# The row of attention scores, moved from in front of the second product to behind it in TensorE's queue

## The chip, the cores and the metric

The kernel runs on one core of one Trainium2 chip. The metric is the device time of one execution in microseconds (us), as the median of several runs. The engines are named as the profile names them: PE is TensorE (its weight loads are listed apart, as PEld), DVE is VectorE, ACT is ScalarE, POOL is GpSimd and SP is SyncE, which issues transfers here.

## What is computed

Four layers stand one behind the other, each with a residual, on an input of 4 batches x 512 rows x 256 columns. The third takes nearly all the arithmetic, the fourth holds the step that is moved.

```python
x = x + L0(x, itok_8)     # adapter 256 -> 64 -> 256, layer norm
x = x + L1(x, itok_7)     # one 256 x 256 product
x = x + L2(x, itok_2)     # five two-layer nets 256 -> 1024 -> 256, gated
x = x + L3(x, itok_2)     # attention pooling

# L2: two chosen experts, mixed with two weights, and three shared nets
dense(x, wi, wo) = relu(x @ wi) @ wo

# L3
attn_in = tanh(hidden @ W1 + b1)          # 512 x 64
scores  = attn_in @ v                     # 512
masked  = where(mask, scores[None, :], -1e30)   # prefix, suffix or all but itself
p       = softmax(masked)
out     = (p @ hidden) / count(mask)
```

## The kernel before

**Precision.** Each factor of a product is split in a high and a low part (names ending in `_hi` and `_lo`), and a product is the sum of three matmuls: high by low, high by high, low by high. So a product over 256 rows of contraction, with 512 columns, is six matmuls.

**Slots.** A batch is worked off in 40 slots (`SLOTS`), one for each 128 hidden units of the five nets. In slot q PE computes the first product of chunk q (`first_product`, six matmuls into `ps_hid`, lines 801, 802, 806), then whatever small steps of other layers belong to the slot, and then the second product of chunk q-2 (`second_product`, six matmuls into `ps_net`, lines 858, 859, 863). ACT turns the first product into `hid_hi` (line 1068) and DVE into `hid_lo` (line 1705). There are three banks for the hidden chunks, so the first product of chunk q waits for `hid_lo` of chunk q-3.

**The small steps.** While batch b goes through its slots, the layers 0 and 1 of batch b+1 (`stage_a`) and the attention of batch b-1 (`stage_c`) are threaded in. The table `C_SLOT` says in which slot each step of the attention stands: the hidden layer of the attention in slot 10, its split in slot 11 (DVE lines 1386 and 1388, which write `att_split`), the row of scores in slot 12, and then on DVE a copy of the scores in column form (lines 1393 and 1396), a running maximum from either side in slots 13 and 14, and so on. The products that need the exponents stand in slots 19, 21 and 22. The attention of the last batch, and the last steps of the one before it, have code of their own behind the loop (`last_rows`).

**The row of scores.** These are two matmuls of 512 columns into `ps_side`, lines 689 and 690. The first contracts over 64 partitions (`att_split[0:A]` with A = 64, against the low part of v), the second over 128 (all of `att_split`, against the high part of v). In front of them stands a wait on DVE for `att_lo`, the end of line 1388. DVE's line 1393 waits for the second. The step is run three times: during the batches 1, 2 and 3, for the batches 0, 1 and 2.

**What sets the order.** Nothing is scheduled. Each engine works its own queue in the order in which the code is written out, and waits on semaphores that count finished steps of other engines. A wait holds everything behind it on its engine. Before the change PE's order in slot 12 is first product of chunk 12, row of scores, second product of chunk 10.

Of the kernel before, what the change touches and what calls it, by code (L numbers as in the profile page):

```python
# [31 lines left out]
def cond_resid_program(  # L32
# [56 lines left out]
    with ExitStack() as ctx:  # L89
# [196 lines left out]
        def score_banks(final):  # L286

            rows = (ps_net[:, 0, 0:HS], ps_hid[:, 0, 0:HS]) if final else (ps_side[:, 1],)
            return rows, ps_hid[:, 2]
# [31 lines left out]
        def ring(b, q):  # L321
            return (b * SLOTS + q) % HB
# [145 lines left out]
        def _(pe):  # L468
# [212 lines left out]
                    product_both(ps_side[:, 0], att_w_st, (c_dve.sem, c_dve.at(i, "x3lo1"))).then_inc(c_pe.sem, 1)  # L681
                attention(slot, i, False)

            def attention(slot, i, final):

                if slot == C_SLOT["scores"]:
                    row = score_banks(False)[0][0]
                    pe.wait_ge(c_dve.sem, c_dve.at(i, "att_lo"))
                    mm(row, att_v_lo[:], att_split[0:A], start=True, stop=False)
                    mm(row, att_v_hi[:], att_split[:], start=False, stop=True).then_inc(c_pe.sem, 1)  # L690
                if slot == (LATE_TSUM if i == LATE else C_SLOT["tsum"]):
                    tile_sums(i, False)
                if 0 <= slot - C_SLOT["out"] < 2 and i != LATE:
                    t = 2 * (slot - C_SLOT["out"])
                    pooled((t, t + 1), i, "loop")
# [7 lines left out]
            def tile_sums(i, final):  # L703


                pe_s, _, dve_s, n = c_steps(i, final)
                _, vh, vl = c_buffers(final)
                pe.wait_ge(dve_s.sem, dve_s.at(n, "edge_lo"))
                if final:
                    pe.wait_ge(e_pool.sem, e_pool.at(0, "val_lo1"))  # L710
                for t in range(R):
                    st = edge_st[:, t * P:(t + 1) * P]
                    mm(tsum_bank(final), st, vh[:, t], start=(t == 0), stop=False)
                    last = mm(tsum_bank(final), st, vl[:, t], start=False, stop=(t == R - 1))
                last.then_inc(pe_s.sem, 1)

            def pooled(tiles, i, mode):


                final = mode == "final"  # L720
                f, half = int(final), tiles[0] // 2
                pe_s, _, dve_s, n = c_steps(i, final)
                _, vh, vl = c_buffers(final)
                part = str(half) if final else ""
                pe.wait_ge(dve_s.sem, dve_s.at(n, "phi" + part if final else "tsum_lo"))
                for t in tiles:
                    if tiles[0] == 2 and mode == "loop":
                        pe.wait_ge(dve_s.sem, dve_s.at(n, f"out{t - 2}"))
                    mm(out_bank(t, mode), prob_hi[:, f, tile_cols(t)], vh[:, t], start=True, stop=False)
                    mm(out_bank(t, mode), prob_hi[:, f, tile_cols(t)], vl[:, t], start=False, stop=False)  # L730
                if final:
                    pe.wait_ge(e_dve.sem, e_dve.at(0, f"plo{half}"))
                for t in tiles:
                    mm(out_bank(t, mode), prob_lo[:, f, tile_cols(t)], vh[:, t], start=False, stop=False)
                if final:
                    pe.wait_ge(e_dve.sem, e_dve.at(0, "tsum_lo"))
                    pe.wait_ge(e_pool.sem, e_pool.at(0, f"wgt_lo{half}"))
                else:
                    pe.wait_ge(c_dve.sem, c_dve.at(n, "wgt_lo"))
                for t in tiles:  # L740
                    mm(out_bank(t, mode), wgt_st[:, f, tile_cols(t)], tsum[:, f], start=False, stop=True).then_inc(pe_s.sem, 1)

            def last_gates(slot):

                if slot == END_GATE:
                    pe.wait_ge(gate_in, 32)
                    pe.wait_ge(gate_sum.sem, gate_sum.at(B - 1, "g2k1"))
                    pe.wait_ge(c_dve.sem, c_dve.at(LATE, "tsum_lo"))
                    pe.wait_ge(e_act.sem, e_act.at(0, "last0"))
                    gate_columns(True).then_inc(e_pe.sem, 1)  # L750
                if slot == END_GATE + 1:
                    pe.wait_ge(e_act.sem, e_act.at(0, "gate_h"))
                    gate_logits().then_inc(e_pe.sem, 1)
# [55 lines left out]
            def bank_free(b, net, k):  # L809


                if k == 1 and (net > 0 or b > 0):
                    by, i, name = evac_act, (b if net > 0 else b - 1), f"g{(net - 1) % NG}"
                elif k == 0 and (net >= 2 or b > 0):
                    by, i, name = evac_dve, (b if net >= 2 else b - 1), f"g{(net - 2) % NG}"
                else:
                    return
                pe.wait_ge(by.sem, by.at(i, name))

            def second_product_halved(b, q):  # L820

                net, tiles, c = NG - 1, chunks(q, True), q % (CH // 2)
                w, half = tiles[0][0] % RING, int(q > HALF0_END)
                if c == 0:
                    bank_free(b, net, half)

                def term(wo, hid, n, k, start=False, stop=False):
                    return mm(ps_net[:, GROUP_BANKS[net][half], k * HS:(k + 1) * HS], wo[:, w, n, k * P:(k + 1) * P], hid[:, ring(b, q), tiles[n][3]],  # L830
                              start=start, stop=stop, skip_group_check=True)

                pe.wait_ge(hid_hi_ready, b * SLOTS + q + 1)
                if split_by_vector(b, tiles[0][0]):
                    pe.wait_ge(end_wo_lo_ready, tiles[0][0] - PAIRS + 3)
                for n in range(2):
                    for k in range(KD):
                        term(wo_hi, hid_hi, n, k, start=(c == 0 and n == 0 and k == 0))
                        term(wo_lo, hid_hi, n, k)
                pe.wait_ge(hid_lo_ready, b * SLOTS + q + 1)  # L840
                for n in range(2):
                    for k in range(KD):
                        last = term(wo_hi, hid_lo, n, k, stop=(c == CH // 2 - 1 and n == 1))
                last.then_inc(net_chunk_done, 1)

            def second_product(b, q, first, halved):

                if halved and q >= SLOTS - CH:
                    return second_product_halved(b, q)
                net, slot = GROUP_AT[q // CH], ring(b, q)  # L850
                opens, closes = q == GROUP_FIRST[net], q == GROUP_END[net] - 1
                pe.wait_ge(hid_hi_ready, b * SLOTS + q + 1)
                w = (q // 2) % RING
                for k in range(KD):
                    if opens:
                        bank_free(b, net, k)
                    cols, dst = slice(k * P, (k + 1) * P), ps_net[:, GROUP_BANKS[net][k]]
                    mm(dst, wo_hi[:, w, q % 2, cols], hid_hi[:, slot], start=opens, stop=False)  # L858
                    mm(dst, wo_lo[:, w, q % 2, cols], hid_hi[:, slot], start=False, stop=False)  # L859
                pe.wait_ge(hid_lo_ready, b * SLOTS + q + 1)  # L860
                for k in range(KD):
                    cols, dst = slice(k * P, (k + 1) * P), ps_net[:, GROUP_BANKS[net][k]]
                    last = mm(dst, wo_hi[:, w, q % 2, cols], hid_lo[:, slot], start=False, stop=closes)  # L863
                last.then_inc(net_chunk_done, 1)

            def batch(b, first, last):
                for q in range(SLOTS):
                    first_product(b, q, first, last)
                    if not first and (not last or q < C_SLOT["out"] or q == LATE_TSUM):
                        stage_c(q, b - 1)  # L870
                    if not last:
                        stage_a(q, b + 1, not first)
                    if last and q == END_GATE:
                        last_gates(q)
                    for s in second_slots(q, last):
                        second_product(b, s, first, last)
                    if last and q == END_GATE:
                        last_gates(q + 1)
                if last:
                    second_product(b, SLOTS - 1, first, last)  # L880
# [1008 lines left out]
```

## Time and profile before

| | |
|---|---|
| median of 3 runs | 525.22 us |
| lowest and highest of them | 524.85, 525.82 us |
| the profiled execution's own time | 524.68 us |
| its span, first to last instruction | 522.9 us |
| mean granted clock of PE | 0.993 |
| PE busy | 509.9 us, 98% of the span |
| PE weight loads | 422.9 us, 81% |
| DVE, ACT, POOL busy | 63%, 51%, 46% |

The profiled execution took 524.68 us, of which 1.8 us lie outside its span. It is 0.54 us below the median. A busy time of PE is not a measure of its useful work here, since the records of neighbouring matmuls overlap. What tells whether PE moved on is the distance from the start of one matmul to the start of the next, and rows of a timeline are read that way below.

### The profile page before, as it was taken

To read this page: it belongs to the slowest core of one execution; us is meant where nothing else is said; L and a number is where in the kernel's file an instruction comes from. 1 tells how busy PE (TensorE), PEld (TensorE's weight loads), DVE (VectorE), ACT (ScalarE), POOL (GpSimd) and SP (SyncE) were. 2 spreads that over 40 slices of the span, in tenths; PEclk is the share of its full clock that TensorE was granted. 3 is DMA by queue.
4 is the path that set the end of the run, shared out by engine and by line. 5 is a ranking of instruction groups with operands and counts; after the bars stand their busy time and mean duration, and the time that the engine had idled before them with its cause. 6 is when DMAs were issued, how large, how long until landed. Compare 5 with 4: busy or idle time off the path is not lost.

```text
span 522.9 us, 7047 instructions
## 1 busy us (share of the span) xinstructions
PE 509.9 (98%) x2463; PEld 422.9 (81%) x2465; DVE 329.5 (63%) x606; ACT 266.1 (51%) x508; POOL 238.5 (46%) x205
## 2 busy tenths in 40 slices
PE   8899999999999999999999999999999999999986
PEld 5688888888888788888888788888888878888974
DVE  7688224884676674786467675687367676435386
ACT  4565554443557563545266564445355647444253
POOL 2655455445344443443535433434544434734034
PEclk9999999999999999999999999999999999999997
DMA  5624442222224323323143422322222223420002
GB/s 172 202 107 132 104 137 102 81 81 81 81 81 131 102 80 88 132 66 113 52 137 97 145 89 81 121 81 80 81 81 81 80 81 104 139 81 1 1 0 81
DMA packets 44539, 49.31 MB, mean 94 GB/s; under 512 B 7380, under 2 KB 34264, under 8 KB 44504
## 3 DMA queue, kind: packets, MB, share of 16 engines
q1 hardware_dynamic: 42888, 47.03, 28.0%
q10 hardware_dynamic: 1616, 1.84, 1.0%
q8 instruction: 20, 0.33, 0.3%
q14 instruction: 15, 0.12, 0.1%
HBM read 46.76 MB, written 2.10 MB: 93 GB/s over the span
## 4 chain that ended last, share of the span: by engine, by line
PE 91%; DVE 5%; ACT 2%; ACTq 1%; POOL 1%; issue 1%; DVEq 0%
PE ps_hid L801 14%; PE ps_hid L806 13%; PE ps_hid L802 13%; PE ps_net L858 13%; PE ps_net L859 13%; PE ps_net L863 13%; PE ps_net L830 2%; PE ps_side L554 1%; PE ps_side L662 1%; PE ps_side L478 1%; PE ps_side L482 1%; PE ps_side L477 1%; DVE att_split L1386 1%; PE ps_side L488 1%; PE ps_side L491 1%; PE ps_side L530 1%
## 5 line engine op out<-in xcount | busy, mean ns | idle before, releaser
L1705 DVE SCALAR_TENSOR_TENSOR hid_lo<-ps_hid,hid_hi 128x512 fp32r<-128x512 f32 x160 | 110.4, 690 | 165.8 <-ACT hid_hi L1068 164.8
L1801 POOL TENSOR_TENSOR wi_lo<-raw_wi,wi_hi 128x512 fp32r<-128x512 f32 x78 | 104.1, 1334 | 225.3 <-ACT wo_hi L1049 121.2
L1068 ACT ACTIVATE hid_hi<-ps_hid 128x512 fp32r<-128x512 f32 x160 | 95.4, 597 | 208.9 <-PE ps_hid L806 208.2
L801 PE MATMUL ps_hid<-x2T_hi,wi_lo 128*128 128x512 f32 (+1 forms) x332 | 125.9, 381 | 0.3 <-POOL wi_lo L1799 0.3
L802 PE MATMUL ps_hid<-x2T_hi,wi_hi 128*128 128x512 f32 (+1 forms) x332 | 125.3, 380 | 0.0
L858 PE MATMUL ps_net<-hid_hi,wo_hi 128*128 128x512 f32 x304 | 120.8, 397 | 0.0
L859 PE MATMUL ps_net<-hid_hi,wo_lo 128*128 128x512 f32 x304 | 118.8, 391 | 0.0
L1802 POOL TENSOR_TENSOR wo_lo<-raw_wo,wo_hi 128x512 fp32r<-128x512 f32 x78 | 101.5, 1301 | 0.0
L806 PE MATMUL ps_hid<-x2T_lo,wi_hi 128*128 128x512 f32 (+1 forms) x332 | 99.1, 380 | 0.0
L863 PE MATMUL ps_net<-hid_lo,wo_hi 128*128 128x512 f32 x304 | 93.9, 390 | 0.0
L801 PEld LDWEIGHTS ps_hid<-x2T_hi,wi_lo 128*128 128x128 f32 x332 | 62.4, 188 | 12.4 <-POOL wi_lo L1799 0.5
L802 PEld LDWEIGHTS ps_hid<-x2T_hi,wi_hi 128*128 128x128 f32 x332 | 62.5, 188 | 11.7
L806 PEld LDWEIGHTS ps_hid<-x2T_lo,wi_hi 128*128 128x128 f32 x332 | 61.3, 188 | 11.8
L863 PEld LDWEIGHTS ps_net<-hid_lo,wo_hi 128*128 128x128 f32 x304 | 57.1, 188 | 12.2
L859 PEld LDWEIGHTS ps_net<-hid_hi,wo_lo 128*128 128x128 f32 x304 | 57.2, 188 | 10.7
L858 PEld LDWEIGHTS ps_net<-hid_hi,wo_hi 128*128 128x128 f32 x304 | 57.2, 188 | 10.7
L1042 ACT ACTIVATE wi_hi<-raw_wi 128x512 fp32r<-128x512 f32 x79 | 49.3, 624 | 0.8 <-PE ps_net L863 0.8
L1049 ACT ACTIVATE wo_hi<-raw_wo 128x512 fp32r<-128x512 f32 x47 | 29.2, 622 | 0.0
L1046 ACT ACTIVATE wo_hi<-raw_wo,par 128x512 fp32r<-128x512 f32 x32 | 22.9, 715 | 1.1 <-DVE mix_done L1539 1.1
L1047 ACT ACTIVATE raw_wo<-raw_wo,par 128x512 f32<-128x512 f32 x32 | 22.8, 712 | 0.0
L1303 DVE SCALAR_TENSOR_TENSOR x3T<-netT,gates,x3T 128x512 f32<-128x512 f32 x24 | 19.6, 855 | 0.1
L1693 DVE SCALAR_TENSOR_TENSOR gate_acc<-gate_w,netT,gate_acc 128x256 f32<-128x256 f32 x26 | 17.5, 672 | 2.1 <-DVE gate_acc L1690 0.5
(324 smaller groups left out, 532.2 us busy)
## 6 DMA issues: line engine op xcount, KB each, us to landing
raw_wi<-in_L_cond_share_wi_dram SPq DMA_DIRECT2D x23, 512.0 KB, 3.7
raw_wo<-in_L_cond_share_wo_dram SPq DMA_DIRECT2D x23, 512.0 KB, 4.8
raw_wi<-in_L_cond_expert_wi_dram SPq DMA_DIRECT2D x16, 512.0 KB, 3.7
raw_wo<-in_L_cond_expert_wo_dram SPq DMA_DIRECT2D x16, 512.0 KB, 4.7
x_rows<-in_x_dram SPq DMA_DIRECT2D x3, 512.0 KB, 5.9
out_dram<-out_rows SPq DMA_DIRECT2D x6, 256.0 KB, 5.1
gate_w<-in_L_cond_gate_w_dram SPq DMA_DIRECT2D x1, 1024.0 KB, 5.5
subj_w<-in_L_cond_weight_dram SPq DMA_DIRECT2D x3, 256.0 KB, 2.7
```

The lines of the kernel that those rows point to most:

```text
L801: mm(dst, wi_lo[:, w, k, c], x2T_hi[:, k, rows], start=(k == 0), stop=False)
L802: mm(dst, wi_hi[:, w, k, c], x2T_hi[:, k, rows], start=False, stop=False)
L806: last = mm(dst, wi_hi[:, w, k, c], x2T_lo[:, k, rows], start=False, stop=(k == KD - 1))
L858: mm(dst, wo_hi[:, w, q % 2, cols], hid_hi[:, slot], start=opens, stop=False)
L859: mm(dst, wo_lo[:, w, q % 2, cols], hid_hi[:, slot], start=False, stop=False)
L863: last = mm(dst, wo_hi[:, w, q % 2, cols], hid_lo[:, slot], start=False, stop=closes)
L1042: fn(wi_hi[:, w], raw_wi[:, half % 2, :, c], ACT.Copy)
L1049: fn(wo_hi[:, w], raw, ACT.Copy).then_inc(w_hi_ready, 1)
L1068: fn(hid_hi[:, ring(b, q)], ps_hid[:, ring(b, q)], ACT.Relu).then_inc(hid_hi_ready, 1)
L1705: v.scalar_tensor_tensor(out=hid_lo[:, ring(b, q)], in0=ps_hid[:, ring(b, q)], scalar=0.0, in1=f32(hid_hi[:, ring(b, q)]), op0=ALU.max, op ...
L1801: g.tensor_tensor(wi_lo[:, w], raw_wi[:, half % 2, :, c], f32(wi_hi[:, w]), ALU.subtract)
L1802: g.tensor_tensor(wo_lo[:, w], raw_wo[:, half % 2, t], f32(wo_hi[:, w]), ALU.subtract).then_inc(w_lo_ready, 1)
```

## The change

The two matmuls and their wait are taken out of `attention` and put into a function of their own. `attention` was called from `stage_c`, ahead of the second product of the slot. The new function is called behind it. The condition `if not first` runs it for the batches 1, 2 and 3, as before. No instruction is added or removed, and no other engine's code is touched.

```diff
-            def attention(slot, i, final):
-
+            def score_row(slot, i):
                 if slot == C_SLOT["scores"]:
                     row = score_banks(False)[0][0]
                     pe.wait_ge(c_dve.sem, c_dve.at(i, "att_lo"))
                     mm(row, att_v_lo[:], att_split[0:A], start=True, stop=False)
                     mm(row, att_v_hi[:], att_split[:], start=False, stop=True).then_inc(c_pe.sem, 1)
+
+            def attention(slot, i, final):
+
...
                     for s in second_slots(q, last):
                         second_product(b, s, first, last)
+                    if not first:
+                        score_row(q, b - 1)
                     if last and q == END_GATE:
                         last_gates(q + 1)
```

PE's queue in slot 12 of batch 1, before the change. In brackets stand the semaphores that an instruction waits for: `c_dve` counts DVE's steps of the attention, `hid_hi_ready` and `hid_lo_ready` the halves of the hidden chunks.

```order
L806 MATMUL ps_hid<-x2T_lo,wi_hi 128x512 x2
L689 MATMUL ps_side<-att_split,att_v_lo 128x512 [waits c_dve]
L690 MATMUL ps_side<-att_split,att_v_hi 128x512
L858 MATMUL ps_net<-hid_hi,wo_hi 128x512 [waits hid_hi_ready]
L859 MATMUL ps_net<-hid_hi,wo_lo 128x512
L858 MATMUL ps_net<-hid_hi,wo_hi 128x512
L859 MATMUL ps_net<-hid_hi,wo_lo 128x512
L863 MATMUL ps_net<-hid_lo,wo_hi 128x512 [waits hid_lo_ready]
L863 MATMUL ps_net<-hid_lo,wo_hi 128x512
L801 MATMUL ps_hid<-x2T_hi,wi_lo 128x512 [waits hid_lo_ready]
```

The same place after the change, where the line numbers are those of the new file (806 has become 808, 689 has become 688, 858 has become 860, 801 has become 803).

```order
L808 MATMUL ps_hid<-x2T_lo,wi_hi 128x512 x2
L860 MATMUL ps_net<-hid_hi,wo_hi 128x512 [waits hid_hi_ready]
L861 MATMUL ps_net<-hid_hi,wo_lo 128x512
L860 MATMUL ps_net<-hid_hi,wo_hi 128x512
L861 MATMUL ps_net<-hid_hi,wo_lo 128x512
L865 MATMUL ps_net<-hid_lo,wo_hi 128x512 [waits hid_lo_ready]
L865 MATMUL ps_net<-hid_lo,wo_hi 128x512
L688 MATMUL ps_side<-att_split,att_v_lo 128x512 [waits c_dve]
L689 MATMUL ps_side<-att_split,att_v_hi 128x512
L803 MATMUL ps_hid<-x2T_hi,wi_lo 128x512 [waits hid_lo_ready]
```

The two matmuls of the row have gone past six matmuls of the second product. They now stand between the second product of chunk 10 and the first product of chunk 13.

DVE's queue at the end of slot 11, in slot 12 and at the start of slot 13, which is the same before and after the change but for line numbers (these are of before).

```order
L1386 CAST att_split<-attT 64x512 [waits c_act]
L1388 TENSOR_TENSOR att_split<-attT,att_split 64x512 [waits c_dve]
L1705 SCALAR_TENSOR_TENSOR hid_lo<-ps_hid,hid_hi 128x512 [waits hid_hi_ready]
L1393 TENSOR_TENSOR prob<-ps_side,ident 128x512 [waits c_pe]
L1396 TENSOR_REDUCE score_col<-prob 128x4 [waits c_dve]
L1705 SCALAR_TENSOR_TENSOR hid_lo<-ps_hid,hid_hi 128x512 [waits hid_hi_ready]
```

Nothing moved there. Line 1393 waits for the row of scores, and behind it in the queue stands `hid_lo` of chunk 13.

## Rows read from the trace of the kernel before

**Rows 1.** The page, part 1: busy us of each engine, share of span, instructions.
```profile
PE 509.9 (98%) x2463; PEld 422.9 (81%) x2465; DVE 329.5 (63%) x606; ACT 266.1 (51%) x508; POOL 238.5 (46%) x205
```
**Rows 2.** What PE waited for, 60 to 480 us: total us, times, longest.
```profile
PE ps_side L689 <- DVE att_split L1388: 1.2, 3, 0.4
```
**Rows 3.** Timeline, PE, slot 12 of batches 1 and 3: start us, duration us, line.
```profile
171.76 0.61 PE L806 MATMUL ps_hid<-x2T_lo,wi_hi 128*128 128x512 f32 x2
172.76 0.50 PE L689 MATMUL ps_side<-att_split,att_v_lo 64*128 64x512 f32 x1 [0.39 <-DVE att_split L1388]
173.19 0.50 PE L690 MATMUL ps_side<-att_split,att_v_hi 128*128 128x512 f32 x1
173.53 0.39 PE L858 MATMUL ps_net<-hid_hi,wo_hi 128*128 128x512 f32 x1
...
418.43 0.62 PE L806 MATMUL ps_hid<-x2T_lo,wi_hi 128*128 128x512 f32 x2
...
420.19 0.39 PE L858 MATMUL ps_net<-hid_hi,wo_hi 128*128 128x512 f32 x1
```
**Rows 4.** Timeline, weight loads, slot 12 of batch 1.
```profile
172.76 0.18 PEld L689 LDWEIGHTS ps_side<-att_split,att_v_lo 64*128 64x128 f32 x1 [0.81 <-DVE att_split L1388]
173.19 0.19 PEld L690 LDWEIGHTS ps_side<-att_split,att_v_hi 128*128 128x128 f32 x1 [0.25 <-issue]
173.30 0.19 PEld L858 LDWEIGHTS ps_net<-hid_hi,wo_hi 128*128 128x128 f32 x1
```
**Rows 5.** Timeline, DVE, slots 11 to 13 of batch 1.
```profile
172.02 0.69 DVE L1388 TENSOR_TENSOR att_split<-attT,att_split 64x512 fp32r<-64x512 f32 x1
...
173.73 0.69 DVE L1393 TENSOR_TENSOR prob<-ps_side,ident 128x512 f32<-128x512 f32 x1
174.45 0.69 DVE L1396 TENSOR_REDUCE score_col<-prob 128x4 f32<-128x512 f32 x1
177.16 0.69 DVE L1705 SCALAR_TENSOR_TENSOR hid_lo<-ps_hid,hid_hi 128x512 fp32r<-128x512 f32 x1 [2.02 <-ACT hid_hi L1068]
```
**Rows 6.** Timeline, PE, the second product of chunk 13 (slot 15).
```profile
181.71 0.39 PE L858 MATMUL ps_net<-hid_hi,wo_hi 128*128 128x512 f32 x1
...
182.62 0.62 PE L863 MATMUL ps_net<-hid_lo,wo_hi 128*128 128x512 f32 x2
```
**Rows 7.** Timeline, PE, a restart after a wait between matmuls of equal partitions.
```profile
483.20 0.39 PE L801 MATMUL ps_hid<-x2T_hi,wi_lo 128*128 128x256 f32 x1 [0.30 <-POOL wi_lo L1799]
483.42 0.28 PE L802 MATMUL ps_hid<-x2T_hi,wi_hi 128*128 128x256 f32 x1
483.54 0.28 PE L801 MATMUL ps_hid<-x2T_hi,wi_lo 128*128 128x256 f32 x1
```
**Rows 8.** Timeline of the last stage, PE and weight loads: four transposes in two surroundings.
```profile
502.35 0.60 PE L662 MATMUL ps_side<-ident,x3T 128*128 128x128 f32 x4
502.70 0.37 PE L729 MATMUL ps_net<-val_hi,prob_hi 128*128 128x258 f32 x1
...
506.76 0.66 PE L662 MATMUL ps_side<-ident,x3T 128*128 128x128 f32 x4
507.35 1.05 PE L700 MATMUL ps_hid<-att_v,attT 64*128 64x1 f32 x8
...
506.76 0.42 PEld L662 LDWEIGHTS ps_side<-ident,x3T 128*128 128x128 f32 x4 [0.33 <-issue]
507.35 0.96 PEld L700 LDWEIGHTS ps_hid<-att_v,attT 64*128 64x128 f32 x8 [0.17 <-issue]
```
**Rows 9.** Stretches: busy PE, PEld, DVE, ACT, POOL; granted clock, DMA. Then PE's timeline.
```profile
508.00:509.00 1.00, 0.40 (x4) 0.31 (x3) 0.96 (x3) 0.62 (x3) 0.54 (x1) 0.89 0.00 0
515.00:516.00 1.00, 1.00 (x6) 0.40 (x4) 0.90 (x4) 1.00 (x4) 0.86 (x2) 0.70 0.00 0
...
510.29 0.42 PE L730 MATMUL ps_net<-val_lo,prob_hi 128*128 128x258 f32 x1
510.50 0.42 PE L729 MATMUL ps_net<-val_hi,prob_hi 128*128 128x258 f32 x1
```

## The prediction, made before the changed kernel was run

> **What bounds the kernel now.** I read the shares of busy time first. PE is busy for 509.9 of 522.9 us, and no other engine passes 63% [rows 1]. So PE's queue sets the time of the loop, and only what makes that queue longer or shorter counts there. The next view is the list of what PE waited for. Between 60 and 480 us, which is nearly the whole of the four batches, it holds one entry: line 689, the first matmul of the row of scores, waits for DVE's line 1388, three times, 1.2 us in all [rows 2]. The reader should see two things. Every other transfer and every other engine is early enough throughout the loop, so there is no second wait standing close behind this one in the list. And what can be won by curing this wait is small.
>
> The list understates the loss, because it counts only the gap between the modelled end of one matmul and the start of the next. The timeline gives the true loss by starts. A matmul of 512 columns in the steady stream starts 0.2275 us after the one before: from the first matmul of line 858 at 181.71 to line 863 at 182.62 are four steps [rows 6]. In slot 12 the first of the two matmuls of line 806 starts at 171.76, and line 858 starts at 173.53 [rows 3]. Between them lie four steps, two of line 806 and two of the row, which at the steady pace would be 0.91 us. They took 1.77 us, 0.86 us too long. The third occurrence reads 418.43 to 420.19, which is 1.76 us, 0.85 too long [rows 3], and the second lies between. So slot 12 loses 0.86 us in each of three batches, 2.6 us in all.
>
> **Where the 0.86 us go.** They fall into parts, and the change touches them differently.
>
> The first part is the wait. Line 689 should start two steps after 171.76, at 172.22, and starts at 172.76 [rows 3], 0.54 us late. DVE's line 1388 ends at 172.02 + 0.69 = 172.71 [rows 5], and the matmul starts 0.05 us after. This is a genuine wait on DVE.
>
> The second part lies behind the wait. Line 690 starts 0.43 us after line 689, and line 858 starts 0.34 us after line 690 [rows 3], in place of 0.23 each: 0.20 and 0.11 us too much, 0.31 together. Some of that belongs to any restart. Where PE restarts after a wait between two matmuls of 128 partitions, the next one comes 0.22 us after it and the following one 0.12 us later [rows 7], so a restart costs 0.10 us, the time in which the weight load lies bare. The remaining 0.21 us are not explained by the restart. They belong to the step from 64 partitions to 128. The weight load of line 690 is not issued while line 689 runs: it stands 0.25 us idle for want of issue, and starts at 173.19 together with its matmul [rows 4], where in the steady stream a load runs one step ahead, as that of line 858 does, at 173.30 for a matmul at 173.53. I read it as 0.10 us of standing still before the load and 0.11 us of bare load.
>
> **The change, part by part.**
>
> *The wait.* In the new place the row comes six matmuls later. The second product of chunk 10 starts at 172.22, since its inputs are two chunks old, and takes 6 x 0.2275 = 1.37 us, so the row is due at 173.58. DVE's line 1388 ends at 172.71, because nothing ahead of it moves. The cover is 173.58 - 172.71 = 0.87 us, and even a weight load issued one step early, at 173.35, finds its data. The wait of 0.54 us goes, three times: -1.62 us. If the cover were gone, the wait would return at its own length, at most the 0.54 us that it has now.
>
> *The restart.* With no wait, the bare load that follows a wait would go too, 0.10 us a time. But it goes only if the load of line 689 may be issued early, and that is the open question, because line 689 uses 64 partitions and stands behind matmuls of 128.
>
> *Going from 128 partitions to 64.* Before the change this price could not be seen, since it lay under the wait. It is now on PE's path. The nearest rows are in the last stage. Four transposes between matmuls of 128 partitions take 0.35 us from their first start to the next matmul (502.35 to 502.70), and the same four between matmuls of 64 partitions take 0.59 us (506.76 to 507.35) [rows 8]. The load behind them stands idle 0.17 us for want of issue, with no wait in the code there. Of the 0.24 us, 0.10 are the bare first load, and 0.14 are lost in going over to 64 partitions. The way back in slot 12 lost 0.10 before its load [rows 4]. So the price is 0.10 to 0.14 us. Its bounds are zero below, if the load is issued early, and 0.33 us above, the idle time of the load at 506.76 [rows 8], which stands behind a slower kind of matmul. I take 0.10 us, the value of this very pair of matmuls. The bare load behind it is then the 0.10 us that the restart costs today, so that term stays.
>
> *Going back from 64 to 128.* Behind line 690 now stands line 801 where line 858 stood. Both are matmuls of 128 partitions with their data ready. The 0.21 us stay as they are: 0.
>
> The Trainium skill has a rule on this. "TensorEngine Tiling (Array Packing)", section Key Properties, says that a change of the tiling mode, and not merely of the tile, drains TensorE. By that rule the row pays at both ends wherever it stands and the forecast below holds; without it the sum would be 0.1 us or more a batch better. The idle loads on both sides of the 64-partition matmuls agree with it.
>
> *DVE.* The row now ends later. In slot 12 it started at 172.76 and starts at 173.58 + 0.10 = 173.68, which is 0.92 us later, and DVE's lines 1393 and 1396 follow it: they end at 174.45 + 0.69 + 0.92 = 176.06. Behind them stands `hid_lo` of chunk 13, which before the change started at 177.16 after 2.02 us of idle time [rows 5], and which now can start 0.44 us earlier, at 176.72. So DVE keeps 0.66 us of idle time there and passes nothing on. All later steps of the attention stand behind a `hid_lo` in DVE's queue and keep their distance to PE.
>
> *The rest.* ACT, POOL, SP and all transfers are paced by PE's finished chunks, and none was late before. They move forward together with PE. The stall of 0.30 us at 483.20 [rows 7] waits for a split on POOL whose own start hangs on a finished chunk, and so keeps its length.
>
> **The sum.** For each batch -0.54 (wait) + 0.10 (over to 64 partitions) = -0.44 us; three batches -1.3 us. The slot lies in the loop, on PE, and PE leads to the last stage, so all of it should reach the end. The profiled execution would go from 524.68 to 523.4 us, its span from 522.9 to 521.6. Taken from the median of the runs, 525.22, the forecast is 523.9 us, 0.25% less.
>
> **The rivals.**
>
> *A. No price for 64 partitions.* All that is lost in slot 12 is a consequence of the wait. Then 0.86 us a batch are won, 2.6 us in all: 522.6 us. With only the entry free, the gain is 0.64 a batch: 523.3 us. For it speaks that the 0.31 us have never been seen apart from a wait. Against it speaks the 0.59 against 0.35 us of the transposes [rows 8]. Chance 0.12.
>
> *B. A higher price.* At the upper bound of 0.33 us a batch, 3 x 0.21 = 0.6 us are left: 524.6 us. The row that gives this bound stands behind matmuls of another kind. Chance 0.12.
>
> *C. The last stage gives it back.* Near the end PE's granted clock falls to half, to 1.2 GHz, when PE idles: it is 0.89 in the stretch of 508 to 509 us, in which PE is busy for 0.40 us, and back on its way up at 0.70 in that of 515 to 516 [rows 9]. In between a matmul of 258 columns starts 0.21 us after the last [rows 9] instead of 0.12 us. Were the return to full clock bound to elapsed time and not to the work, the work would come 1.3 us earlier against it, and some or all of the last 16 matmuls, two pairs of tiles with 8 each, would run at half clock: 8 to 16 x 0.09 = 0.7 to 1.4 us back, to 524.6 to 525.3, say 524.9 us. The spread of the runs, 524.85 to 525.82 us, may already contain it, in which case it changes no median. Chance 0.12.
>
> *D. The change does not do what it says.* The wait would have to last on in the new place, or PE to find another of the same length behind it. The queues show the row behind the second product, the cover is 0.87 us, and no other wait is in the list [rows 2]. It would give 525.2 us. Chance 0.05.
>
> *E. Slower.* DVE now waits longer for the row, with `hid_lo` of chunk 13 behind that wait. If this made `hid_lo` late, PE's second product of chunk 13 would stand. Before, `hid_lo` ended at 177.85 and was needed at 182.62 [rows 5, 6], 4.8 us later, and 2.0 us of idle time lie before it. It decides from a delay of some 6 us, against 0.9 us that I find. Were the delay one slot more than that, 2.7 us in each batch, the time would be 525.2 + 8.2 - 1.6 = 531.8 us. Chance 0.04.
>
> **How the numbers follow.** The forecast has 0.55, A 0.12, B 0.12, C 0.12, D 0.05, E 0.04. The range leaves out the far half of A, and D and E but for their edge: 523.1 to 525.0 us. A measurement of this kernel can tell about 0.2% from no change, which is 1.05 us, so faster means below 524.17. The forecast is 0.27 us beyond that line; I give 0.50 of its 0.55 to faster, add A, and have 0.62. Same gets the other 0.05, B, C and D: 0.34. Slower gets E: 0.04.
>
> **What would show it.** In the list of what PE waited for, the row's entry is gone and nothing new of this size has come. In PE's timeline the second product starts 0.23 us after the last matmul of the first, and the row's first matmul 0.33 us after the last of the second product (0.23 would be A, 0.56 would be B), its second 0.43 us after that, and line 801 of the next chunk 0.34 us later (both 0.23 in A). The load of the row's first matmul shows idle time for want of issue. DVE's line 1393 waits for the row and 1396 ends about 0.7 us before the next `hid_lo`. The stretches of half clock near the end have the same place relative to the work; if they do not, C is at work. The prediction is wrong if the row's surroundings lose more than 0.5 us a batch, or if the loop ends 1.3 us earlier and the kernel does not.

## The result, and the profile after

| | before | after |
|---|---|---|
| median | 525.34 us (6 runs) | 523.63 us (6 runs) |
| lowest and highest | 524.85, 525.82 us | 523.46, 524.20 us |
| span of the profiled execution | 522.9 us | 521.4 us |
| mean granted clock | 0.993 | 0.993 |

The ratio of the times is 0.9968 with a 95% interval from 0.9957 to 0.9980. The change makes the kernel faster by 1.7 us, or 0.32%, and the interval of 1.1 to 2.3 us holds the 1.3 us of the forecast. The median of 523.63 us lies 0.3 us below the 523.9 us of the forecast, inside its range of 523.1 to 525.0 us.

In the changed file the row of scores has the lines 688 and 689, the first product 803, 804 and 808, the second 860, 861 and 865. PE's timeline in slot 12 of batch 1, which answers to [rows 3], reads as follows (start us, duration us, line):

```profile
173.00 0.61 PE L865 MATMUL ps_net<-hid_lo,wo_hi 128*128 128x512 f32 x2
173.55 0.49 PE L688 MATMUL ps_side<-att_split,att_v_lo 64*128 64x512 f32 x1
173.97 0.50 PE L689 MATMUL ps_side<-att_split,att_v_hi 128*128 128x512 f32 x1
174.31 0.39 PE L803 MATMUL ps_hid<-x2T_hi,wi_lo 128*128 128x512 f32 x1
```

From the first matmul of line 865 to line 803 are four steps, which at the steady pace of 0.2275 us take 0.91 us. They took 1.31 us, 0.40 too long. Before, the four steps around the row were 0.86 us too long. The row's first matmul should start at 173.455 and starts 0.10 us late. The next steps are 0.42 and 0.34 us; before they were 0.43 and 0.34.

The list of what PE and its weight loads waited for, 60 to 480 us, shows no entry of PE any more in place of [rows 2]. It has three entries of the weight loads (total us, times, longest), of which the last two are the row's:

```profile
PEld ps_side L554 <- DVE norm L1217: 1.3, 3, 0.4
PEld ps_side L688 <- issue: 1.1, 3, 0.4
PEld ps_side L689 <- issue: 0.7, 3, 0.2
```

"Issue" means that no semaphore explains the idle time: the data of line 688 were ready, and its load was still not sent ahead. On DVE, against [rows 5], the row is now waited for, and the idle time ahead of `hid_lo` of chunk 13 has shrunk from 2.02 to 0.67 us without being used up:

```profile
171.91 0.69 DVE L1392 TENSOR_TENSOR att_split<-attT,att_split 64x512 fp32r<-64x512 f32 x1
...
174.51 0.69 DVE L1397 TENSOR_TENSOR prob<-ps_side,ident 128x512 f32<-128x512 f32 x1 [0.83 <-PE ps_side L689]
175.24 0.69 DVE L1400 TENSOR_REDUCE score_col<-prob 128x4 f32<-128x512 f32 x1
176.59 0.69 DVE L1709 SCALAR_TENSOR_TENSOR hid_lo<-ps_hid,hid_hi 128x512 fp32r<-128x512 f32 x1 [0.67 <-ACT hid_hi L1072]
```

Where the 1.5 us between the two spans come from can be read from the start of the same matmul in both traces. Line 806 of slot 12 in batch 1 starts at 171.76 in [rows 3] and its counterpart at 171.65: 0.11 us arise in the part ahead of any changed instruction. That is chance: over all profiles of this document, in which PE's work up to there is the same, the start lies between 171.62 and 171.92 us. The first transposes of the last stage start at 502.35 in [rows 8] and now here:

```profile
500.86 0.60 PE L662 MATMUL ps_side<-ident,x3T 128*128 128x128 f32 x4
```

That is 1.49 us earlier. Less the 0.11 us, three slots gave 1.38 us, 0.46 each, which is 0.86 - 0.40. From there on both take 20.5 us to the end of the span.

### The profile page after: what moved, and what is told of

It reads as the page before. It is cut to its first block, busy times and chain, and to the rows that moved or that the text cites. A ratio compares the mean times of both kernels' runs of the same rounds, so it can differ in the third digit from the quotient of the medians.

```text
span 521.4 us, 7049 instructions
## 1 busy us (share of the span) xinstructions
PE 509.6 (98%) x2465; PEld 422.3 (81%) x2465; DVE 329.8 (63%) x606; ACT 266.1 (51%) x508; POOL 238.5 (46%) x205
## 4 chain that ended last, share of the span: by engine, by line
PE 93%; DVE 3%; ACT 1%; ACTq 1%; POOL 1%; issue 0%; DVEq 0%
PE ps_hid L803 14%; PE ps_hid L808 14%; PE ps_hid L804 14%; PE ps_net L860 13%; PE ps_net L861 13%; PE ps_net L865 13%; PE ps_net L832 2%; PE ps_side L554 1%; PE ps_side L662 1%; PE ps_side L478 1%; PE ps_side L482 1%; PE ps_side L477 1%; PE ps_side L488 1%; PE ps_side L491 1%; PE ps_side L530 1%
```

## The experiments

The theory after the result: the wait of 0.54 us is gone, and what is left of the row's loss, 0.40 us a batch, is the price of going from matmuls over 128 partitions to one over 64 and back. Rivals are that the place itself matters, that the loss has another cause, and that DVE's lateness has a price.

The ratios below are against runs of the kernel before that were made beside each experiment. Their medians are 525.34 us for the first four experiments, 524.99 us for those with five pairs or ten grouped matmuls, and 525.15 us for the last, with matmuls on zeros.

**The row's first matmul over 128 partitions.** The low part of v gets zeros in its upper 64 partitions, and the matmul reads all of `att_split`. The sums stay the same.

```diff
-        att_v_lo = sb("att_v_lo", [A, P], F32R)
+        att_v_lo = sb("att_v_lo", [P, P], F32R)
...
-                    mm(row, att_v_lo[:], att_split[0:A], start=True, stop=False)
+                    mm(row, att_v_lo[:], att_split[:], start=True, stop=False)
...
+            v.memset(f32(att_v_lo[A:P]), 0.0)
```

> The changed kernel, with the row's first matmul over 128 partitions instead of 64: the low part of v is padded with zeros in the upper 64, so the count of matmuls and the sums stay as they are. Theory (in the changed kernel 0.40 us a batch are lost because the array goes from 128 partitions to 64 and back): both idle loads vanish, the row's matmuls start 0.23 us apart like all others, and 3 x 0.40 = 1.2 us are won over the changed kernel: 522.4 us, ratio to the kernel before 0.9944. Rival (the loss comes from something else about the row, its place, its bank or its operands): 523.6 us, ratio 0.9968, and the 0.10, 0.20 and 0.11 us stay.

Measured: 522.73 us (6 runs), ratio 0.9948, interval 0.9936 to 0.9961. In slot 12 nothing is lost any more:

```profile
173.09 0.61 PE L865 MATMUL ps_net<-hid_lo,wo_hi 128*128 128x512 f32 x2
173.54 0.39 PE L688 MATMUL ps_side<-att_split,att_v_lo 128*128 128x512 f32 x1
173.78 0.39 PE L689 MATMUL ps_side<-att_split,att_v_hi 128*128 128x512 f32 x1
174.01 0.39 PE L803 MATMUL ps_hid<-x2T_hi,wi_lo 128*128 128x512 f32 x1
```

The four steps take 0.92 us, and the loads' two entries for the row are gone from the list. The last stage begins at 499.64 us, 1.22 us earlier than in the changed kernel, as the theory has it. The rival is out. The time fell by only 0.9 us and the span by 0.5; the last part of this section comes back to that.

**The same padding with the row in its old place**, in front of the second product.

> The kernel before, with the row in its old place but with 128 partitions in both of its matmuls (low part of v padded with zeros). It separates the wait from the change of partitions. Theory: the wait of 0.54 us and the bare load of the restart, 0.10 us, stay, the 0.21 us behind them go: 3 x 0.21 = 0.65 us less than before, 524.7 us, ratio 0.9988. Rival A (all that is lost in slot 12 follows from the wait): as before, 525.3 us, with 0.43 and 0.34 us between the starts. Rival (padding does not help): the same.

Measured: 524.92 us (11 runs), ratio 0.9993, interval 0.9984 to 1.0002. The time alone, which fits the forecast of 0.9988, doesn't tell it from no change. The trace does:

```profile
171.92 0.61 PE L806 MATMUL ps_hid<-x2T_lo,wi_hi 128*128 128x512 f32 x2
172.92 0.50 PE L689 MATMUL ps_side<-att_split,att_v_lo 128*128 128x512 f32 x1 [0.39 <-DVE att_split L1388]
173.26 0.39 PE L690 MATMUL ps_side<-att_split,att_v_hi 128*128 128x512 f32 x1
173.49 0.40 PE L858 MATMUL ps_net<-hid_hi,wo_hi 128*128 128x512 f32 x1
```

The wait is the old one: line 689 starts 0.54 us behind its time. The step after it is 0.34 us, 0.11 more than the pace, and the next one 0.23. So a restart costs 0.11 us, and the 0.21 us of before that are missing here belong to the partitions. From line 806 of slot 12 in batch 1 to the last stage this kernel takes 330.03 us (171.92 to 501.95), the kernel before 330.59 us (171.76 to 502.35), so 0.56 us went where 0.65 were expected. Rival A of the prediction, in which everything followed from the wait, is out.

**The row one slot later, in its old position between the two products.**

```diff
-                if slot == C_SLOT["scores"]:
+                if slot == C_SLOT["scores"] + 1:
```

> The kernel before, with the row in its old position between first and second product, but one slot later, 13 instead of 12, so that DVE has long finished its part. It takes the wait away without going behind the second product. Theory (only the wait counted, the place does not): as the changed kernel, 523.6 us, ratio 0.9968, 0.40 us lost in slot 13. DVE gets the row 1.4 us later than in the changed kernel, hid_lo of chunk 13 comes about 0.7 us late and PE does not notice, since it has 4.8 us. Rival (lateness on DVE already costs, or the place behind the second product is itself of worth): 524.5 us or more.

Measured: 523.60 us (6 runs), ratio 0.9968, interval 0.9956 to 0.9980, the same as the changed kernel. The four steps around the row, from 174.44 to 175.74, take 1.30 us. `hid_lo` of chunk 13 starts at 177.27 on DVE, 0.7 us later than in the changed kernel, with no idle time ahead of it:

```profile
177.27 0.68 DVE L1705 SCALAR_TENSOR_TENSOR hid_lo<-ps_hid,hid_hi 128x512 fp32r<-128x512 f32 x1
```

PE waits for nothing between 60 and 480 us. So the gain lies in asking for `att_lo` later, and the place behind the second product has no worth of its own.

**The row three slots later, between the two products of slot 15.** The edit is the same with `+ 3`.

> The kernel before, with the row between first and second product of slot 15, three slots late, so that hid_lo of chunk 13 is queued on DVE behind a wait for a row that stands right ahead of the matmuls which need it. It tests the slower rival of the prediction. Theory: the row ends about 7 us after its time in the changed kernel; hid_lo of chunk 13 ends 1.4 us after PE's line 863 of that chunk asks for it; with the restart 1.5 us are lost a batch, 4.4 in all, over the 523.6 us of the changed kernel: 528.0 us. Rival (DVE's lateness passes nothing to PE): 523.6 us. Rival (it also makes ACT late in slot 16 and costs a second stall): 530 us or more.

Measured: 527.97 us (2 runs), ratio 1.0045, interval 1.0028 to 1.0063. PE's waits from 60 to 490 us, the line of interest:

```profile
PE ps_net L863 <- DVE hid_lo L1705: 3.5, 3, 1.2
```

PE's timeline in slot 15 of batch 1:

```profile
180.82 0.50 PE L690 MATMUL ps_side<-att_split,att_v_hi 128*128 128x512 f32 x1
...
181.86 0.39 PE L859 MATMUL ps_net<-hid_hi,wo_lo 128*128 128x512 f32 x1
183.43 0.73 PE L863 MATMUL ps_net<-hid_lo,wo_hi 128*128 128x512 f32 x2 [1.18 <-DVE hid_lo L1705]
184.00 0.40 PE L801 MATMUL ps_hid<-x2T_hi,wi_lo 128*128 128x512 f32 x1
```

DVE's timeline there shows its wait for the row, and `hid_lo` of chunk 13 behind it, which ends at 183.37:

```profile
181.36 0.69 DVE L1393 TENSOR_TENSOR prob<-ps_side,ident 128x512 f32<-128x512 f32 x1 [7.63 <-PE ps_side L690]
...
182.69 0.68 DVE L1705 SCALAR_TENSOR_TENSOR hid_lo<-ps_hid,hid_hi 128x512 fp32r<-128x512 f32 x1
```

Line 863 starts 1.34 us behind its time (183.43 - 181.86 - 0.23) and the step after its pair is 0.11 us too long: 1.45 us a batch, 4.4 in all. The last stage begins at 505.20 against 500.86 us, 4.34 us later. So the slower rival of the prediction is a real mechanism with the size that the queue of DVE gives. It costs nothing one slot later than the original place and 1.45 us a batch three slots later; in between nothing was run. An estimate from these rows: line 690 comes 7.7 us later than in the kernel before (180.82 against 173.19, with 0.06 us for the earlier start of slot 12 here), and 1.34 us of that reach PE, so the loss would begin at a delay of about 6.3 us.

**The price of a pair by itself.** The row is computed five times in a row, with 64 and 128 partitions in turn, and the same with 128 throughout.

```diff
+                    for _ in range(4):
+                        mm(row, att_v_lo[:], att_split[0:A], start=True, stop=False)
+                        mm(row, att_v_hi[:], att_split[:], start=False, stop=True)
                     mm(row, att_v_lo[:], att_split[0:A], start=True, stop=False)
```

> The changed kernel with the row computed five times in a row, each time a matmul over 64 partitions and one over 128. It measures the price of a pair by itself. Theory (each passage between 64 and 128 partitions keeps the next weight load from running ahead): a further pair costs 0.455 us of steady pace and 0.31 us of lost time or more, up to 0.42; four further pairs in three batches 12 x 0.77 to 12 x 0.87 = 9.2 to 10.4 us: 532.8 to 534.1 us. Rival (lost time comes only once per row): 12 x 0.455 = 5.5 us, 529.1 us.

> The same with 128 partitions in every matmul (low part of v padded with zeros). Theory: the steady pace alone, 12 x 0.455 = 5.5 us over the padded kernel with one row, 522.4 + 5.5 = 527.9 us. Rival (the row's matmuls are slow for another reason): as the kernel with five unpadded pairs, 533 us.

Measured: 534.91 us (2 runs), ratio 1.0186, interval 1.0156 to 1.0215, for pairs of 64 and 128; 528.04 us (3 runs), ratio 1.0055, interval 1.0033 to 1.0078, for 128 throughout. Two steps of the first, then three of the second:

```profile
174.05 0.50 PE L690 MATMUL ps_side<-att_split,att_v_hi 128*128 128x512 f32 x1
174.48 0.49 PE L689 MATMUL ps_side<-att_split,att_v_lo 64*128 64x512 f32 x1
174.90 0.50 PE L690 MATMUL ps_side<-att_split,att_v_hi 128*128 128x512 f32 x1
```

```profile
174.03 0.39 PE L689 MATMUL ps_side<-att_split,att_v_lo 128*128 128x512 f32 x1
174.25 0.40 PE L690 MATMUL ps_side<-att_split,att_v_hi 128*128 128x512 f32 x1
174.49 0.39 PE L689 MATMUL ps_side<-att_split,att_v_lo 128*128 128x512 f32 x1
```

A matmul over 64 partitions behind one over 128 starts 0.43 us after it, and so does one over 128 behind one over 64; between equal ones it is 0.23 us. A passage costs 0.20 us, a pair 0.85 us. Twelve further pairs would be 10.2 us. The last stage begins 10.35 us later than in the changed kernel. The median lies 11.3 us above that kernel's and 0.8 us above the expected range. The profiled execution spent 21.5 us in its last stage instead of 20.5, of which more below. The kernel with 128 partitions throughout came out at 528.04 us where 527.9 was expected, and its last stage begins 5.64 us later than in the padded kernel with one row.

**Ten matmuls, two passages.** The same ten matmuls a batch as in the first of these, grouped: four over 128 partitions, five over 64, one over 128.

```diff
+                    for _ in range(4):
+                        mm(row, att_v_hi[:], att_split[:], start=True, stop=True)
+                    for _ in range(4):
+                        mm(row, att_v_lo[:], att_split[0:A], start=True, stop=True)
```

> The changed kernel with the same ten matmuls as in the five pairs, but grouped: four over 128 partitions, then five over 64, then one over 128. Theory (what costs is the passage, not a matmul over 64 partitions): only two passages a batch as in the changed kernel, so eight further matmuls at steady pace, 12 x 0.455 = 5.5 us: 529.1 us. Rival (every matmul over 64 partitions loses time): as the five pairs, 533 us.

Measured: 528.77 us (3 runs), ratio 1.0071, interval 1.0047 to 1.0096. The five matmuls over 64 partitions (line 691 four times, then 692) and their neighbours:

```profile
173.53 1.09 PE L689 MATMUL ps_side<-att_split,att_v_hi 128*128 128x512 f32 x4
174.54 1.21 PE L691 MATMUL ps_side<-att_split,att_v_lo 64*128 64x512 f32 x4
175.59 0.39 PE L692 MATMUL ps_side<-att_split,att_v_lo 64*128 64x512 f32 x1
175.92 0.50 PE L693 MATMUL ps_side<-att_split,att_v_hi 128*128 128x512 f32 x1
176.25 0.39 PE L807 MATMUL ps_hid<-x2T_hi,wi_lo 128*128 128x512 f32 x1
```

From 173.53 to 176.25 are ten steps, 2.28 us at the steady pace, in 2.72 us. The 0.44 us too much are nearly the 0.40 of a single row, though five matmuls run over 64 partitions. It is the passage that costs, and not the matmul over 64.

Not every change in the number of partitions has this price. In the kernel before, matmuls over 97 and over 128 partitions, with 256 columns, stand in turn elsewhere, and they start 0.12 us apart, as those with 256 columns over 128 partitions do in [rows 7]:

```profile
99.05 0.28 PE L516 MATMUL ps_side<-w_lo,hT_hi 97*128 97x256 f32 x1
99.17 0.29 PE L517 MATMUL ps_side<-w_hi,hT_both 128*128 128x256 f32 x1
99.30 0.28 PE L516 MATMUL ps_side<-w_lo,hT_hi 97*128 97x256 f32 x1
```

**The last stage.** In its profile the padded kernel had won 1.22 us by the start of its last stage and only 0.5 us in its span. Two kernels were profiled once more, unaltered.

> The padded kernel with the row behind the second product once more, for a second look at its last stage. In its first profile the half-clock stretch began 5.4 us after the last stage's first matmul over 64 partitions, in the kernel before and the changed one after 3.3 us, and the last stage took 21.3 us in place of 20.5. Theory (where the half-clock stretch falls is chance of the execution, not a trait of the kernel): either picture may come; if the early one comes (3.3 us, last stage 20.5 us), the span is 520.2 us. Rival (the row's earlier end always shifts the work against the clock): the late one again, span 520.9 us.

> The changed kernel, unaltered, once more, for a second look at slot 12 and at the last stage. Theory: slot 12 to the hundredth as in its first profile (0.40 us lost a batch); last stage 20.5 us with the clock falling 3.3 us after the first matmul over 64 partitions, or, by chance, 21.3 us with it falling at 5.4 us. Rival: the same picture of the clock each time.

Measured, with the start of the first transposes of the last stage, the length from there to the end of the span, and the places where PE's granted clock falls to its half, 1.2 GHz, and where it is full again:

| kernel | last stage starts | length | clock falls | full again | span | time |
|---|---|---|---|---|---|---|
| before | 502.35 | 20.5 | 508.8 | 515.6 | 522.9 | 524.68 |
| changed | 500.86 | 20.5 | 507.3 | 514.2 | 521.4 | 524.20 |
| changed, again | 500.82 | 20.8 | 508.2 | 515.0 | 521.6 | 523.49 |
| padded | 499.64 | 21.3 | 508.1 | 514.9 | 520.9 | 522.71 |
| padded, again | 499.75 | 20.8 | 506.9 | 513.8 | 520.5 | 522.30 |

The loop is the same to 0.1 us from one execution to the next: in its second profile the changed kernel again needs 1.30 us for the four steps around the row. The last stage is not the same. The next rows are PE's restart after its 1.5 us of idle time, and the stretches between 507 and 509 us, in the padded kernel. Behind the stretch stand its length, the busy times of PE, PEld, DVE, ACT and POOL with their counts, and then the granted clock. The first profile:

```profile
507.20 0.39 PE L731 MATMUL ps_net<-val_hi,prob_hi 128*128 128x258 f32 x1 [1.51 <-ACT norm L1020]
...
507.00:508.00 1.00, 0.80 (x6) 0.80 (x7) 0.93 (x4) 0.15 (x1) 0.68 (x1) 1.00 0.00 0
508.00:509.00 1.00, 0.60 (x4) 0.31 (x2) 0.90 (x6) 0.20 (x1) 0.00 (x0) 0.54 0.00 0
```

The second:

```profile
507.30 0.58 PE L731 MATMUL ps_net<-val_hi,prob_hi 128*128 128x258 f32 x1 [1.51 <-ACT norm L1020]
...
507.00:508.00 1.00, 0.70 (x3) 0.70 (x4) 0.93 (x4) 0.25 (x1) 0.78 (x1) 0.50 0.00 0
508.00:509.00 1.00, 1.00 (x7) 1.00 (x6) 0.90 (x6) 0.21 (x1) 0.00 (x0) 0.50 0.00 0
```

The work in these two is at the same place to 0.1 us, and the clock falls 1.1 us apart. The places are worked out from the mean in a stretch, with 1.00 ahead of the fall and 0.50 behind it: 0.54 granted between 508 and 509 us puts the fall at 508.1 in the first profile, and 0.97 granted between 506 and 507 us puts it at 506.9 in the second. In the two profiles of the changed kernel it falls 0.9 us apart.

The table shows two things more. Where the clock falls later it is also full again later, by the same amount to 0.1 us, though the work has not moved: 0.8 us between the profiles of the changed kernel, 1.1 us between those of the padded one. And the later in the last stage the clock is full again, the longer the stage: 13.3 us into it in the first two rows, then 14.2, 15.3 and 14.0, with lengths of 20.5, 20.5, 20.8, 21.3 and 20.8 us. So the length differs between executions of one kernel, by 0.3 and 0.5 us in these two. Over all the profiles it lies between 20.5 and 21.5 us, and the 21.3 and 21.5 of two kernels with five pairs are of this kind too, full again at 15.5 and 15.7 us. Expected was one of two pictures; the second profiles showed two others between them, so the choice of two was wrong. What sets the point of the fall was not settled.

A single profile is therefore a poor measure of the whole time. The spans of all runs, not only the profiled ones, have medians of 523.1 us before (the 17 runs beside the first experiments), 521.7 us changed and 520.6 us padded. By spans the change gives 1.4 us and the padding 1.1 us more, which fit the 1.38 and 1.22 us that the traces show in the loop. The times scatter more than the spans, since 1.8 to 2.9 us lie outside the span.

To see whether PE's idle time causes the fall, seven matmuls on zeros were put into it, on top of the padding.

```diff
                 score_columns(col, e_pe)
+                keep_warm(7, ps_hid[:, 1])
                 pe.wait_ge(e_act.sem, e_act.at(0, "late1"))
```

> The padded kernel with the row behind the second product, and seven matmuls on zeros in the last stage, ahead of the pooling of the last but one batch, where PE stands idle for 1.5 us waiting on ACT. They fill that idle time at 0.21 us each. Theory (PE's idle time there is what makes its clock fall to half): the half-clock stretch vanishes or begins later, matmuls of 258 columns behind it start 0.12 us apart instead of 0.21, and the last stage takes 20.0 to 20.5 us in every run: 521.7 to 522.3 us, with a smaller spread than 1 us. Rival (the fall has another cause, or DVE alone sets the last stage): no change against the padded kernel, 522.7 us, with the same spread.

Measured: 522.36 us (4 runs, 522.06 to 522.64), ratio 0.9947, interval 0.9930 to 0.9964. The granted clock by stretches, and PE's longest wait that is left there:

```profile
505.00:512.00 7.00, 6.00 (x38) 4.14 (x38) 6.28 (x19) 4.78 (x15) 3.60 (x5) 1.00 0.00 0
512.00:516.00 4.00, 2.81 (x17) 1.98 (x15) 3.77 (x11) 1.53 (x5) 3.19 (x4) 0.99 0.22 70
516.00:520.00 4.00, 0.00 (x0) 0.00 (x0) 1.24 (x5) 0.00 (x0) 0.00 (x0) 0.50 0.59 197
...
509.50 0.39 PE L715 MATMUL ps_net<-wi_hi,edge_st 128*128 128x258 f32 x1 [1.00 <-DVE edge_st L1373]
```

The clock stays full until PE has no work left. All four runs show it: their mean granted clock is 0.996 to 0.999, against 0.991 to 0.993 in the padded kernel's six. The matmuls of 258 columns start 0.12 us apart. So the fall hangs on that idle time of 1.5 us; the 1.0 us of idle time that is left, up to 509.50, brought none.

The time hardly shows it. The last stage took 20.6 us in the profile, for PE now waits for DVE, 1.0 us there and 0.8 us in three later waits, where the padded kernel's first profile has one such wait, of 0.8 us. Both the time and the last stage are 0.1 us above what was expected. Against the runs beside them the two kernels are not told apart, with ratios of 0.9947 and 0.9948. The spread of the times is 0.6 us in 4 runs against 2.1 us (522.02 to 524.11) in 6, but one run makes up more than half of the 2.1, and without it the spread is 0.9 us. That the spread became smaller is not shown.

## Why the prediction was right

**The wait.** The sum rested on 0.54 us of wait in each of three batches, read from starts and not from the listed idle time of 0.39. All three are gone. The cover was 0.85 us (line 1392 ends at 172.60, the row is due at 173.455), where 0.87 was worked out.

**The price that could not be seen before.** For going from 128 to 64 partitions the prediction took 0.10 us from the way back of the same pair, between bounds of 0 and 0.33. The changed kernel shows 0.10. The four extra pairs show that both directions cost the same, 0.20 us with the bare load. That agrees with what the prediction cites from the Trainium skill, "TensorEngine Tiling (Array Packing)", section Key Properties, that a change of mode drains TensorE: ten grouped matmuls with two passages lose 0.44 us, and five alternating pairs with ten passages lose 1.99 us (173.08 to 177.80, less twelve steps of 0.2275). That a drain is what holds the load back, by 0.10 us, is a reading of the page's rule; the runs show only that the load comes late.

**The term that stays.** The 0.31 us behind the wait were split into 0.10 for the restart and 0.21 for the partitions, from one restart elsewhere [rows 7]. The padded row in its old place showed just this: 0.11 for the restart, and the rest gone.

**DVE.** Lines 1397 and 1400 ended 0.67 us ahead of the next `hid_lo`; 0.66 was worked out.

**The rivals.** A, no price for 64 partitions, is refuted by the padded row in both places. B, a price of 0.33 us, is refuted by the 0.10 in the trace. C, the half clock in the last stage, has a sound core: the return to full clock moved with the fall and not with the work, and a later return went with a longer stage. What C left out is that the fall itself moves, by 0.9 and 1.1 us between executions of the same kernel. In the two profiles that were compared, fall and return came at the same work, and that both last stages took 20.5 us is luck. D is out, since PE's list of waits is empty. E is a real mechanism, with a price of 1.45 us a batch three slots late, and its threshold of some 6 us is 6.3 by the estimate above. The 531.8 us given for E take off the whole wait of 1.6 us and leave out the 0.3 us that the forecast adds for the entry; with them it is 532.1.

**The size.** Forecast was 1.3 us, measured 1.7 with an interval of 1.1 to 2.3 us. The trace gives 1.38 us in the three slots, 0.46 each instead of 0.44. The difference of 1.7 us between the medians of the times is larger than what the loop gives, and by the medians of the spans it is 1.4 us. The 0.3 us between the two would then lie outside the span, which varies between executions, and they are within the interval. The profiled execution of the changed kernel shows this scatter best: it has the shortest span of the six, 521.4 us, and the longest time, 524.20 us. That the measured 1.7 us agree with the 1.3 us as they do rests on the loop for 1.4 us and on chance for the rest.

## What to carry to other kernels

On an engine that is otherwise always busy, a wait of half a microsecond can be cured by asking later, if the work that moves ahead of it is ready and the engine that gets the result later has idle time ahead of its next urgent step. What the list of waits names is less than what is lost: count starts against the steady pace, and split the excess into the wait, the restart and what belongs to the shapes of the matmuls, since the last stays when the wait goes. Here the restart stayed too, because the next load was still held back by the passage to 64 partitions. The shapes were as easily cured: 64 more partitions of zeros in the weight tile gave 0.40 us a batch, nearly as much as the change itself.

## What the runs showed of the hardware that was not expected

- A passage between matmuls over 64 and over 128 partitions costs 0.20 us in either direction (starts 0.43 us apart instead of 0.23, ten passages in a row), even if all operands are ready. Matmuls over 64 among themselves keep nearly the pace of 0.23 us: four of them took 1.05 us to the next, in which the bare load of the first lies. Matmuls over 97 and 128 partitions in turn show no such price (starts 0.12 us apart with 256 columns).
- PE's clock in one kernel fell to half at different points of the work in different executions, with the same 1.5 us of idle time in all: 507.3 and 508.2 us in the changed kernel, 506.9 and 508.1 in the padded one. It was full again later or earlier by the same amount to 0.1 us, and the last stage took between 20.5 and 21.3 us with it. Filling the idle time kept the clock full until PE's work was done, which did not lower the time by more than the noise.
